# Attention values of the tail keys as 32 by 32 blocks in every chunk of both layers, added on VectorE

## The chip, the cores and the metric

The kernel runs on one core of a Trainium2 chip. The metric is device time in microseconds (us), the median of several runs of the whole program; lower is better.

## The reference

Two layers, each a cross attention and a feed-forward network, gated into a residual stream x of 2 batches by 2048 rows by 512 columns, all in float32:

```python
x = x + tanh(g_xattn[l]) * xattn_l(layernorm(x), ctx)
x = x + tanh(g_ffn[l]) * ffn_l(layernorm(x))
```

The context has 154 keys; there are 16 heads of 32 columns. The first layer's attention has no mask. The second has a mask per query and key and normalises the projected queries, keys and values over 512 columns:

```python
scores = einsum('bhqd,bhkd->bhqk', q, k) / sqrt(32)   # layer 1: where(mask == 0, -1e9, scores)
ctx = einsum('bhqk,bhkd->bhqd', softmax(scores), v)
```

The change touches the product of the softmax with v alone.

## The kernel before

**Tiling.** A layer takes 4096 query rows in 8 chunks of 512 (`NCH`), four per batch; the index of a chunk is `it`, and `it + 1`, `it - 1` are the chunks whose queries and outputs are made beside it. The layer without mask is called plain, the one with mask and head normalisation masked (`norm` in the code). Of the 154 keys 128 are main keys and 26 are tail keys. Heads are taken in four tiles of four (`KT` tiles, `t`; `GH` heads, `j`). A product in float32 precision is three passes of rounded high and low parts (`hi_lo_matmul`, L69); "q0" to "q3" in the prediction are the four tiles of `q_front`, 12 matmuls of 128x512 each. Transposed scores with a main key per partition are "S0" to "S3" (`scores_main`, L1535 and L1538), the products with v "V0" to "V3" (`values_of`, L1552 to L1569), with the softmax sums beside them.

**Tail keys.** `scores_tail` (L1506) makes the tail scores of all 16 heads as 16 blocks of 32 by 32, packed so that a head's 26 tail keys lie in one of four row groups of 32 partitions of one of four tiles; `exps_tail` (L715) on ScalarE (ACT) gives `p_tail`. `keys.v_tail` holds the tail values with zeros where a row belongs to another head, so that `values_of` can take one head's tail with all 128 rows of `p_tail` (L1552), four matmuls of 128 rows by 32 columns, into the PSUM bank `values`, on which the four main products (L1556) are added:

```python
nc.tensor.matmul(values[own, :], keys.v_tail[:, b, t, own], p_tail[:, t, :],
                 start=True, stop=False, skip_group_check=True)
```

`c_evict` (L729, ACT) copies `values` to `c_sb` in SBUF, one tile at a time (there is one `values` bank). VectorE (DVE) multiplies `c_sb` by the reciprocal sums that TensorE (PE) has transposed into two banks (`recips`, L1598; `c_back` L1016 plain, `c_mult` L1025 masked), ACT rounds the high part (`cT_back`, L744), and DVE makes the low part (`c_low`/`lo_of`, L1033). That is the input of the output product `y_back` (L69 with wd).

**PSUM.** Four score banks `score[:, 0..3, :]` are used for S0, S1, S2, S3 in turn, `j` for `j`: a bank is free again when ACT's exponential (`exps_main`, L722) has read it. In the masked layer the banks are first filled with the mask (`seed_main`: j = 0, 1, 2 on DVE, L966, and j = 3 on ACT, L707), and PE accumulates on that. Two banks `bank[0], bank[1]` carry in turn the q tiles, `recips`, `qT_front` and `y_back`; in the masked layer `recips(0,1)` need that DVE has taken q tiles 0 and 1 out of them (`q_rows`, L986).

**The order** is written out by hand, one program per engine, with semaphores. PE's program per chunk, before:

```python
q_front(it + 1, (0,)); scores_main(it, 0); q_front(it + 1, (1,)); scores_main(it, 1)
if norm and it: recips(it - 1, (0, 1))
values_of(it, 0); q_front(it + 1, (2, 3)); scores_main(it, 2); values_of(it, 1)
if norm and it: recips(it - 1, (2, 3))
scores_main(it, 3)
```

Then come V2, V3 and the 16 key-maximum products `max_of` (L1479; masked also L1477), from the third on with a `y_back` group of the chunk before behind each. `max_of` m waits until DVE has reduced max m − 2 (L1009), and the first `y_back` for `c_low` of all four tiles. The max of each query is taken before its exponentials of the next chunk. GpSimd (POOL) widens the reciprocals and adds the gate's bias to a residual tile (`add_bias`, L538); DVE's `mask_front` (L948) unpacks the mask for the maxima.

## Time and profile before

| | |
|---|---|
| median of 3 runs | 2413.8 us (2412.69 to 2415.39) |
| profiled execution, its own time | 2415.25 us |
| its span in the trace | 2413.5 us |
| mean granted TensorE clock | 0.989 |
| busy: DVE, ACT, POOL | 1505.3, 1179.1, 238.7 us |
| a plain chunk from 218.36 us on, a masked chunk from 1360.12 us on | 51.01 us, 54.71 us |

The profile is of one execution, so its rows are set against its own time. Busy times overlap across engines. A row of a timeline gives the start, the busy time of a group of like instructions, the engine, the line and the operation, out<-in; in brackets stands the idle time before it with what ended it. A float32 matmul that is not split leaves two records, so "x8" with L1552 are four matmuls. A granted clock of 1.00 is 2.4 GHz, 0.50 is 1.2 GHz.

### The profile page before, as it was taken

What the parts mean: (1) busy time and instruction counts of PE and PEld (TensorE: products, weight loads), DVE (VectorE), ACT (ScalarE), POOL (GpSimd) and SP (SyncE); (2) the same over time, 40 slices, a digit from 0 to 9 for tenths busy, and PEclk for the clock granted to TensorE, in tenths of its full rate; (3) what the DMA queues carried; (4) which work ended last, traced back from release to release, by engine and by line L of the source; (5) the groups of instructions that cost most, each with busy time, mean ns of one, the idle gap of its engine ahead of it and who ended that gap; (6) DMA issues with size and microseconds to landing.
All of it is one profiled execution on the core that took longest, in us unless ns stands there. A gap on an engine that the chain in (4) does not pass through costs nothing.

```text
span 2413.5 us, 32717 instructions
## 1 busy us (share of the span) xinstructions
PE 2354.9 (98%) x12984; PEld 1795.5 (74%) x12984; DVE 1505.3 (62%) x2466; ACT 1179.1 (49%) x1914; POOL 238.7 (10%) x219
## 2 busy tenths in 40 slices
PE   6999999999999999999988999999999999999998
PEld 5566666688888888888765666666788888888886
DVE  5566666442222222223488888886887988988986
ACT  4454544442222222223245566666666666666665
POOL 1012112210000000000211111113000000000000
PEclk9999999999999999999998999999999999999999
DMA  3121112421101101102311121124301011010110
GB/s 129 36 88 53 53 53 70 162 88 53 35 18 53 52 1 53 53 1 87 121 63 50 67 67 67 67 71 140 110 26 46 36 35 35 36 42 29 36 36 18
DMA packets 89143, 140.95 MB, mean 58 GB/s; under 512 B 5024, under 2 KB 27936, under 8 KB 88992
## 3 DMA queue, kind: packets, MB, share of 16 engines
q1 hardware_dynamic: 88992, 138.87, 17.0%
q8 instruction: 103, 1.69, 0.3%
q14 instruction: 48, 0.39, 0.1%
HBM read 105.30 MB, written 33.55 MB: 58 GB/s over the span
## 4 chain that ended last, share of the span: by engine, by line
PE 39%; DVE 8%; ACT 2%; issue 2%; POOL 0%; DVEq 0%; ACTq 0%
PE l_lay_bank L69 19%; PE l_lay_score L69 11%; PE l_lay_score L1479 1%; PE l_lay_score L1535 1%; PE l_lay_score L1552 1%; DVE l_at_at_next L1084 1%; PE l_lay_score L1556 1%; PE l_lay_score L1564 1%; DVE l_at_h_lo L1098 1%; PE l_lay_bank L1395 1%; DVE l_at_at_next L1077 1%; DVE l_at_full L1073 1%; DVE l_at_full L1066 1%; DVE l_at_xTf_lo L972 1%; DVE l_at_maxes L1009 1%
## 5 line engine op out<-in xcount | busy, mean ns | idle before, releaser
L69 PE MATMUL l_lay_score<-l_at_tw_hi,l_at_h_hi 128*128 128x512 f32 x1024 | 401.4, 392 | 5.2 <-DVE l_at_h_lo L1098 4.7
L69 PE MATMUL l_lay_bank<-l_at_xTf_hi,l_at_tw_hi 128*128 128x512 f32 x1024 | 400.1, 391 | 0.0
L69 PE MATMUL l_lay_score<-l_at_tw_hi,l_at_h_lo 128*128 128x512 f32 x1024 | 398.7, 389 | 0.0
L69 PE MATMUL l_lay_score<-l_at_tw_lo,l_at_h_hi 128*128 128x512 f32 x1024 | 398.5, 389 | 0.0
L69 PE MATMUL l_lay_bank<-l_at_xTf_hi,l_at_tw_lo 128*128 128x512 f32 x1024 | 398.5, 389 | 0.0
L69 PE MATMUL l_lay_bank<-l_at_xTf_lo,l_at_tw_hi 128*128 128x512 f32 x1024 | 398.4, 389 | 0.0
L1058 DVE TENSOR_TENSOR l_at_h_lo<-l_at_full,l_at_h_hi 128x512 fp32r<-128x512 f32 x128 | 94.2, 736 | 468.5 <-ACT l_at_h_hi L762 468.5
L757 ACT ACTIVATE l_at_full<-l_lay_bank,l_at_lay_b 128x512 f32<-128x512 f32 x128 | 88.3, 690 | 457.8 <-PE l_lay_bank L69 457.8
L69 PEld LDWEIGHTS l_lay_score<-l_at_tw_hi,l_at_h_hi 128*128 128x128 f32 x1024 | 192.3, 188 | 49.2 <-DVE l_at_h_lo L1098 10.2
L69 PEld LDWEIGHTS l_lay_score<-l_at_tw_hi,l_at_h_lo 128*128 128x128 f32 x1024 | 192.2, 188 | 40.2
L69 PEld LDWEIGHTS l_lay_bank<-l_at_xTf_hi,l_at_tw_lo 128*128 128x128 f32 x1024 | 192.2, 188 | 40.1
L69 PEld LDWEIGHTS l_lay_bank<-l_at_xTf_hi,l_at_tw_hi 128*128 128x128 f32 x1024 | 192.3, 188 | 40.0 <-issue 0.7
L69 PEld LDWEIGHTS l_lay_bank<-l_at_xTf_lo,l_at_tw_hi 128*128 128x128 f32 x1024 | 192.3, 188 | 39.3
L69 PEld LDWEIGHTS l_lay_score<-l_at_tw_lo,l_at_h_hi 128*128 128x128 f32 x1024 | 192.3, 188 | 38.8
L1009 DVE TENSOR_REDUCE l_at_maxes<-l_lay_score 128x4 f32<-128x616 f32 x256 | 197.7, 798 | 27.6 <-PE l_lay_score L1479 24.9
L722 ACT ACTIVATE l_at_p_main<-l_lay_score 128x512 f32<-128x512 f32 x256 | 131.6, 601 | 106.1 <-PE l_lay_score L1538 106.1
L783 ACT ACTIVATE l_at_at_grid<-l_at_at_grid,l_at_lay_grid_bias 128x512 f32<-128x512 f32 x128 | 92.6, 724 | 149.9 <-DVE l_at_at_grid L1088 149.9
L1479 PE MATMUL l_lay_score<-l_at_k_bd,l_at_qT_hi 128*128 128x308 f32 x512 | 131.8, 343 | 6.2 <-ACT l_lay_score L695 3.3
L769 ACT ACTIVATE l_at_grid<-l_at_full,l_at_lay_grid_bias 128x512 f32<-128x512 f32 x128 | 92.0, 719 | 89.2 <-DVE l_at_full L1066 89.2
L1098 DVE SCALAR_TENSOR_TENSOR l_at_h_lo<-l_at_at_grid,l_at_h_hi 128x512 fp32r<-128x512 f32 x128 | 88.1, 688 | 57.0 <-ACT l_at_h_hi L788 57.0
L669 ACT ACTIVATE l_at_xT_hi<-l_lay_bank 128x512 fp32r<-128x512 f32 x64 | 36.6, 596 | 177.7 <-PE l_lay_bank L1395 177.7
L1479 PEld LDWEIGHTS l_lay_score<-l_at_k_bd,l_at_qT_hi 128*128 128x128 f32 x512 | 95.5, 198 | 36.6 <-DVE l_at_maxes L1009 9.7
(195 smaller groups left out, 4063.2 us busy)
## 6 DMA issues: line engine op xcount, KB each, us to landing
both_x_in<-stream SPq DMA_DIRECT2D x25, 1024.0 KB, 5.6
l_at_xg<-stream SPq DMA_DIRECT2D x23, 1024.0 KB, 5.5
stream<-l_at_xg SPq DMA_DIRECT2D x22, 1024.0 KB, 4.3
l_at_tw_raw<-in_l_w SPq DMA_DIRECT2D x64, 256.0 KB, 5.6
both_x_in<-in_x SPq DMA_DIRECT2D x9, 1024.0 KB, 7.7
l_at_xg<-in_x SPq DMA_DIRECT2D x7, 1024.0 KB, 5.4
out<-l_at_xg SPq DMA_DIRECT2D x7, 1024.0 KB, 4.3
l_at_maskT_in<-in_maskT SPq DMA_DIRECT2D x16, 256.0 KB, 3.2
```

The costliest lines, as they stand in the source:

```text
L69: done = nc.tensor.matmul(out, lhs[a], rhs[b], start=first and n == 0, stop=last and n == len(passes) - 1)
L669: nc.scalar.activation((xT if i < NCH else xTf)[0][:, k, :], (bank if i <= NCH else tr)[k % 2][:, :], ACT.Copy)\
L722: nc.scalar.activation(p_main[:, t % 2, j, :], score[:, j, :], ACT.Exp)\
L757: nc.scalar.activation(full[u % 2][:, :], hid[u % 2][:, :], ACT.Relu, bias=b1[:, u % MT:u % MT + 1]).then_inc(h_full, 1)
L769: nc.scalar.activation(grid[u % 2][:, :], full[u % 2][:, :], ACT.Identity, bias=grid_bias[:, 2:3]).then_inc(gridded, 1)
L783: nc.scalar.activation(at_grid[u % AB][:, :], at_grid[u % AB][:, :], ACT.Identity, bias=grid_bias[:, 3:4]).then_inc(rounded, 1)
L972: nc.vector.tensor_tensor(to[1][:, k, :], ps[k % 2][:, :], to[0][:, k, :].bitcast(F32), ALU.subtract)\
L1009: nc.vector.tensor_reduce(to, heads, AX.X, ALU.max).then_inc(max_done, 1)
L1058: nc.vector.tensor_tensor(h[1][u % HB][:, :], full[u % 2][:, :], h[0][u % HB][:, :].bitcast(F32), ALU.subtract)\
L1066: nc.vector.tensor_scalar(full[u % 2][:, :], hid[u % 2][:, :], b1[:, u % MT:u % MT + 1], ROUND_IN, ALU.add, ALU.add)\
L1098: nc.vector.scalar_tensor_tensor(h[1][u % HB][:, :], at_grid[u % AB][:, :], -ROUND_256, h[0][u % HB][:, :].bitcast(F32), ALU.add, ALU.subt ...
L1479: done = nc.tensor.matmul(to, qT_of(it)[0][:, t, q * P:(q + 1) * P], keys.bd[:, b, t, 2 * a:2 * a + 2, :], start=not norm, stop=True, skip ...
```

## The change

`tail_values(it)` is a new PE step, once per chunk: 16 matmuls of 32 rows by 32 columns, each taking only the row group where its head's tail keys are. Tile 0 goes to the bank `values`, on which V0 then accumulates; tiles 1 to 3 go to score banks 1 to 3. `tail_values_out` copies these to `c_sb`, tile 1 on DVE and 2 and 3 on ACT, before S0 or its seeds may use the banks. `values_of` makes only the main products, and for tiles 1 to 3 `c_add` on DVE replaces `c_evict`: `c_sb = values + c_sb`. In the masked layer the seeds are split two on DVE and two on ACT, and the q rows are taken in halves around the new step. The plain layer has q1 ahead of S0, q2 ahead of S1 and q3 ahead of S2. The last chunks, which have no next queries, get the feed-forward network's first products in the place of q0 and q1, and S0 and S1 stand side by side.

```diff
...
                 act.wait_ge(maskT_done, 2 * it + 2)
-                act.wait_ge(exp_done, NS * it + GH * t + GH)
-                nc.scalar.activation(score[:, GH - 1, :], mask_main[:, it % 2, :], ACT.Copy)\
-                    .then_inc(act_seeded, 1)
+                for j in (2, 3):
+                    act.wait_ge(exp_done, NS * it + GH * t + j + 1)
+                    if t == 0:
+                        act.wait_ge(tail_v_act, 2 * it + j - 1)
+                    nc.scalar.activation(score[:, j, :], mask_main[:, it % 2, :], ACT.Copy)\
+                        .then_inc(act_seeded, 1)
 
...
 
+            def tail_values_out(it, t):
+                act.wait_ge(tail_v_ps, 3 * it + t)
+                if it >= 2:
+                    act.wait_ge(cT_lo, KT * (it - 2) + t + 1)
+                nc.scalar.activation(c_sb[:, it % 2, t, :], score[:, t, :], ACT.Copy).then_inc(tail_v_act, 1)
+
             def c_evict(it, t):
...
                 exps_tail(it)
-                if norm:
-                    seed_main(it, 0)
                 if it < B:
                     v_tail_of(it)
-                if not norm:
+                if norm:
+                    tail_values_out(it, 2)
+                    tail_values_out(it, 3)
+                    seed_main(it, 0)
+                else:
                     if more:
...
                         relu_hi(0)
-                exps_main(it, 0)
-                if norm:
-                    seed_main(it, 1)
-                if not norm:
+                    tail_values_out(it, 2)
+                    tail_values_out(it, 3)
                     if more:
...
                         relu_hi(1)
+                exps_main(it, 0)
+                if norm:
+                    seed_main(it, 1)
+                if more and not norm:
+                    q_front(it + 1, (2,))
                 exps_main(it, 1)
...
                 if more and not norm:
-                    q_front(it + 1, (2, 3))
+                    q_front(it + 1, (3,))
                 exps_main(it, 2)
...
                     seed_main(it, 3)
-                c_evict(it, 1)
                 if it and norm:
...
                     front.round_hi(act, "wd")
-                c_evict(it, 2)
                 if more and norm:
...
                     q_front(it + 1, (1,))
-                c_evict(it, 3)
                 if more and norm:
...
                 dve.wait_ge(maskT_done, 2 * it + 2)
-                for j in range(GH - 1):
+                for j in range(2):
                     dve.wait_ge(exp_done, NS * it + GH * t + j + 1)
+                    if t == 0 and j == 1:
+                        tail_values_out(it, 1)
+                        dve.wait_ge(tail_v_dve, it + 1)
                     nc.vector.tensor_copy(score[:, j, :], mask_main[:, it % 2, :]).then_inc(dve_seeded, 1)
...
 
+            def tail_values_out(it, t):
+                dve.wait_ge(tail_v_ps, 3 * it + t)
+                if it >= 2:
+                    dve.wait_ge(cT_lo, KT * (it - 2) + t + 1)
+                nc.vector.tensor_copy(c_sb[:, it % 2, t, :], score[:, t, :]).then_inc(tail_v_dve, 1)
+
+            def c_add(it, t):
+                c = c_sb[:, it % 2, t, :]
+                if t == 1:
+                    dve.wait_ge(tail_v_dve, it + 1)
+                else:
+                    dve.wait_ge(tail_v_act, 2 * it + t - 1)
+                dve.wait_ge(c_ps, KT * it + t + 1)
+                nc.vector.tensor_tensor(c, values, c, ALU.add).then_inc(c_out, 1)
+
             def c_back(it, ts):
...
                     c = c_sb[:, it % 2, t, :]
+                    dve.wait_ge(c_out, u + 1)
                     dve.wait_ge(rT_ps, u + 1)
...
                     c = c_sb[:, it % 2, t, :]
+                    dve.wait_ge(c_out, KT * it + t + 1)
                     dve.wait_ge(rT_ps, KT * it + t + 1)
...
                         done = hi_lo_matmul(nc, bank[t % 2][:, :], lhs, rhs, k == 0, k == KT - 1)
-                    done.then_inc(q_ps, 1)
+                    if ks[-1] == KT - 1:
+                        done.then_inc(q_ps, 1)
 
...
                         if i == 0:
-                            if not norm:
+                            if not norm and t == 0 and j == 1:
+                                pe.wait_ge(tail_v_dve, it + 1)
+                            elif not norm and t == 0 and j > 1:
+                                pe.wait_ge(tail_v_act, 2 * it + j - 1)
+                            elif not norm:
                                 pe.wait_ge(exp_done, NS * it + GH * t + j + 1)
-                            elif j < GH - 1:
-                                pe.wait_ge(dve_seeded, 3 * (KT * it + t) + j + 1)
                             else:
-                                pe.wait_ge(act_seeded, KT * it + t + 1)
+                                pe.wait_ge(dve_seeded if j < 2 else act_seeded,
+                                           2 * (KT * it + t) + j % 2 + 1)
                         nc.tensor.matmul(score[:, j, :], k2[a][rows[j], b, t, 0:P], q2[c][rows[j], t, :],
...
 
+            def tail_values(it):
+                b = it // CPB
+                pe.wait_ge(exp_done, NS * it + KT)
+                if it:
+                    pe.wait_ge(c_out, KT * it)
+                else:
+                    pe.wait_ge(kv_bias, 8)
+                if it % CPB == 0:
+                    pe.wait_ge(v_placed, V_COPIES * (b + 1))
+                for t in range(KT):
+                    for j in range(GH):
+                        c = own_rows[group_of(t, j)]
+                        to = score[own_rows[j], t, :] if t else values[own_rows[j], :]
+                        done = nc.tensor.matmul(to, keys.v_tail[c, b, t, own_rows[j]], p_tail[c, t, :],
+                                                start=True, stop=t > 0, skip_group_check=True)
+                    if t:
+                        done.then_inc(tail_v_ps, 1)
+
             def values_of(it, t):
...
                     pe.wait_ge(kv_bias, 8)
-                if t == 0 and it % CPB == 0:
-                    pe.wait_ge(v_placed, V_COPIES * (b + 1))
-                for j in range(GH):
-                    own = slice(DH * j, DH * (j + 1))
-                    nc.tensor.matmul(values[own, :], keys.v_tail[:, b, t, own], p_tail[:, t, :],
-                                     start=True, stop=False, skip_group_check=True)
                 for j in range(GH):
...
                                             keys.v_main[:, b, DH * head:DH * (head + 1)],
-                                            p_main[:, t % 2, j, :], start=False, stop=True,
+                                            p_main[:, t % 2, j, :], start=t > 0, stop=True,
                                             skip_group_check=True)
...
                 if more:
-                    q_front(it + 1, (0,))
+                    q_front(it + 1, (0,), (0, 1) if norm else range(KT))
                 else:
                     first_product(0)
-                scores_main(it, 0)
-                if more:
+                tail_values(it)
+                if more and norm:
+                    q_front(it + 1, (0,), (2, 3))
+                    q_front(it + 1, (1,), (0, 1))
+                elif more:
                     q_front(it + 1, (1,))
...
                     first_product(1)
-                scores_main(it, 1)
+                scores_main(it, 0)
+                if more:
+                    q_front(it + 1, (1,) if norm else (2,), (2, 3) if norm else range(KT))
                 if norm and it:
                     recips(it - 1, (0, 1))
+                scores_main(it, 1)
                 values_of(it, 0)
                 if more:
-                    q_front(it + 1, (2, 3))
+                    q_front(it + 1, (2, 3) if norm else (3,))
                 scores_main(it, 2)
```

The rest of the diff does the same for the last chunk, and puts `c_add` into DVE's program, which its order shows.

DVE, masked layer, a middle chunk, from the seeds for S3 (`L966 CAST`, then `L981`) to the first maxima, before:

```order
L966 CAST l_lay_score<-l_at_mask_main 128x512 x3
L1000 TENSOR_SCALAR l_at_qn<-l_at_qn,l_at_lay_q_mv,l_at_lay_q_rstd 128x512 x4
L1025 TENSOR_TENSOR l_at_c_sb<-l_at_c_sb,l_lay_bank 128x512 x2
L1033 TENSOR_TENSOR l_at_xT_lo<-l_at_c_sb,l_at_xT_hi 128x512 x2
L940 TENSOR_SCALAR both_x_in<-both_x_in,l_at_lay_mv,l_at_lay_rstd 128x512 x4
L1033 TENSOR_TENSOR l_at_xT_lo<-l_at_c_sb,l_at_xT_hi 128x512 x2
L980 TENSOR_TENSOR l_at_qT_lo<-l_at_q_0,l_at_qT_hi 128x512
L980 TENSOR_TENSOR l_at_qT_lo<-l_at_q_1,l_at_qT_hi 128x512
L1009 TENSOR_REDUCE l_at_maxes<-l_lay_score 128x4 x7
```

and with the change (`L1015` is `q_norm_apply`, `L1057` `c_mult`, `L1065` `c_low`, `L952` `norm_apply`, `L995` `q_low`, `L1024` a maximum):

```order
L981 CAST l_lay_score<-l_at_mask_main 128x512 x2
L1039 TENSOR_TENSOR l_at_c_sb<-l_lay_score,l_at_c_sb 128x512
L1015 TENSOR_SCALAR l_at_qn<-l_at_qn,l_at_lay_q_mv,l_at_lay_q_rstd 128x512 x4
L1057 TENSOR_TENSOR l_at_c_sb<-l_at_c_sb,l_lay_bank 128x512 x2
L1065 TENSOR_TENSOR l_at_xT_lo<-l_at_c_sb,l_at_xT_hi 128x512 x2
L1039 TENSOR_TENSOR l_at_c_sb<-l_lay_score,l_at_c_sb 128x512
L952 TENSOR_SCALAR both_x_in<-both_x_in,l_at_lay_mv,l_at_lay_rstd 128x512 x4
L1065 TENSOR_TENSOR l_at_xT_lo<-l_at_c_sb,l_at_xT_hi 128x512 x2
L1039 TENSOR_TENSOR l_at_c_sb<-l_lay_score,l_at_c_sb 128x512
L995 TENSOR_TENSOR l_at_qT_lo<-l_at_q_0,l_at_qT_hi 128x512
L995 TENSOR_TENSOR l_at_qT_lo<-l_at_q_1,l_at_qT_hi 128x512
L1024 TENSOR_REDUCE l_at_maxes<-l_lay_score 128x4 x7
```

One cast has gone, and three additions (L1039) stand between the steps ahead of the first maximum.

PE, masked layer, a middle chunk, the second half of q1 to V0, before:

```order
L69 MATMUL l_lay_bank<-l_front_wq_hi,l_at_xT_hi 128x512
L69 MATMUL l_lay_bank<-l_front_wq_lo,l_at_xT_hi 128x512
L69 MATMUL l_lay_bank<-l_front_wq_hi,l_at_xT_lo 128x512
L1535 MATMUL l_lay_score<-l_at_qT_hi,l_at_k_hi 128x512 x4
L1535 MATMUL l_lay_score<-l_at_qT_lo,l_at_k_hi 128x512 x4
L1535 MATMUL l_lay_score<-l_at_qT_hi,l_at_k_lo 128x512 x4
L1538 MATMUL l_lay_score<-l_at_negT,l_at_pick 128x512 x4
L1598 MATMUL l_lay_bank<-ident,l_at_r_wide 128x128 x8
L1552 MATMUL l_lay_score<-l_at_p_tail,l_at_v_tail 32x512 x4
L1556 MATMUL l_lay_score<-l_at_p_main,l_at_v_main 32x512 x4
L1564 MATMUL l_lay_score<-l_at_p_main,l_at_e_main 32x512 x4
```

and with the change (`L1586`, `L1589` are `scores_main`, `L1661` `recips`):

```order
L69 MATMUL l_lay_bank<-l_front_wq_hi,l_at_xT_hi 128x512
L69 MATMUL l_lay_bank<-l_front_wq_lo,l_at_xT_hi 128x512
L69 MATMUL l_lay_bank<-l_front_wq_hi,l_at_xT_lo 128x512
L1661 MATMUL l_lay_bank<-ident,l_at_r_wide 128x128 x8
L1586 MATMUL l_lay_score<-l_at_qT_hi,l_at_k_hi 128x512 x4
L1586 MATMUL l_lay_score<-l_at_qT_lo,l_at_k_hi 128x512 x4
L1586 MATMUL l_lay_score<-l_at_qT_hi,l_at_k_lo 128x512 x4
L1589 MATMUL l_lay_score<-l_at_negT,l_at_pick 128x512 x4
L1619 MATMUL l_lay_score<-l_at_p_main,l_at_v_main 32x512 x4
L1627 MATMUL l_lay_score<-l_at_p_main,l_at_e_main 32x512 x4
```

`recips` has moved ahead of S1, and the tail product (L1552) has gone from V0.

DVE, plain layer, a middle chunk, from `norm_apply` to the maxima, before:

```order
L940 TENSOR_SCALAR both_x_in<-both_x_in,l_at_lay_mv,l_at_lay_rstd 128x512 x4
L1016 TENSOR_TENSOR l_at_c_sb<-l_at_c_sb,l_lay_bank 128x512 x2
L1033 TENSOR_TENSOR l_at_xT_lo<-l_at_c_sb,l_at_xT_hi 128x512 x2
L1016 TENSOR_TENSOR l_at_c_sb<-l_at_c_sb,l_lay_bank 128x512 x2
L1033 TENSOR_TENSOR l_at_xT_lo<-l_at_c_sb,l_at_xT_hi 128x512 x2
L1009 TENSOR_REDUCE l_at_maxes<-l_lay_score 128x4 x8
```

and with the change (`L1047` is `c_back`):

```order
L952 TENSOR_SCALAR both_x_in<-both_x_in,l_at_lay_mv,l_at_lay_rstd 128x512 x4
L1039 TENSOR_TENSOR l_at_c_sb<-l_lay_score,l_at_c_sb 128x512
L1047 TENSOR_TENSOR l_at_c_sb<-l_at_c_sb,l_lay_bank 128x512 x2
L1065 TENSOR_TENSOR l_at_xT_lo<-l_at_c_sb,l_at_xT_hi 128x512 x2
L1039 TENSOR_TENSOR l_at_c_sb<-l_lay_score,l_at_c_sb 128x512
L1047 TENSOR_TENSOR l_at_c_sb<-l_at_c_sb,l_lay_bank 128x512 x2
L1065 TENSOR_TENSOR l_at_xT_lo<-l_at_c_sb,l_at_xT_hi 128x512 x2
L1024 TENSOR_REDUCE l_at_maxes<-l_lay_score 128x4 x3
L1039 TENSOR_TENSOR l_at_c_sb<-l_lay_score,l_at_c_sb 128x512
L1024 TENSOR_REDUCE l_at_maxes<-l_lay_score 128x4 x5
```

The three additions stand ahead of the first `c_back`, between the two, and behind the third maximum.

## Rows read from the trace of the kernel before

**Rows 1.** The page, busy time by engine
```profile
PE 2354.9 (98%) x12984; PEld 1795.5 (74%) x12984; DVE 1505.3 (62%) x2466; ACT 1179.1 (49%) x1914; POOL 238.7 (10%) x219
```

**Rows 2.** Windows, one steady chunk of each layer: us, busy and count by engine, clock, DMA
```profile
218.36:269.37 51.01, 50.95 (x377) 33.78 (x376) 32.50 (x50) 23.19 (x42) 8.15 (x7) 1.00 0.17 63
1360.12:1414.83 54.71, 54.58 (x418) 36.05 (x417) 47.75 (x82) 33.18 (x58) 9.73 (x9) 1.00 0.22 75
```

**Rows 3.** Timeline of PE, plain chunk: start, busy time of the group, instruction
```profile
220.01 1.14 PE L1506 MATMUL l_lay_score<-l_at_q,l_at_k_tail 32*32 32x512 f32 x32
221.08 1.09 PE L1395 MATMUL l_lay_bank<-ident,both_x_in 128*128 128x128 f32 x8
231.59 0.40 PE L1538 MATMUL l_lay_score<-l_at_negT,l_at_pick 32*128 32x512 f32 x4
231.92 1.07 PE L1552 MATMUL l_lay_score<-l_at_p_tail,l_at_v_tail 128*32 128x512 f32 x8
232.80 1.04 PE L1556 MATMUL l_lay_score<-l_at_p_main,l_at_v_main 128*32 128x512 f32 x8
241.14 0.51 PE L1535 MATMUL l_lay_score<-l_at_qT_hi,l_at_k_hi 32*128 32x512 f32 x4
```

**Rows 4.** Timeline of ACT, DVE and PE, same chunk, its second half
```profile
242.59 2.04 ACT L722 ACTIVATE l_at_p_main<-l_lay_score 128x512 f32<-128x512 f32 x4
246.29 2.06 ACT L722 ACTIVATE l_at_p_main<-l_lay_score 128x512 f32<-128x512 f32 x4 [1.16 <-PE l_lay_score L1538]
250.55 1.28 DVE L1016 TENSOR_TENSOR l_at_c_sb<-l_at_c_sb,l_lay_bank 128x512 f32<-128x512 f32 x2 [0.36 <-PE l_lay_bank L1598]
251.94 1.29 DVE L1033 TENSOR_TENSOR l_at_xT_lo<-l_at_c_sb,l_at_xT_hi 128x512 fp32r<-128x512 f32 x2
253.15 2.40 DVE L1009 TENSOR_REDUCE l_at_maxes<-l_lay_score 128x4 f32<-128x616 f32 x3
254.16 0.55 PE L1479 MATMUL l_lay_score<-l_at_k_bd,l_at_qT_hi 128*128 128x308 f32 x2
```

**Rows 5.** Timeline of PE, masked chunk: q row 2, max 2
```profile
1378.68 0.49 PE L69 MATMUL l_lay_bank<-l_front_wq_hi,l_at_xT_hi 128*128 128x512 f32 x1
1399.04 0.30 PE L1477 MATMUL l_lay_score<-l_at_mask_add,ident_bf 128*128 128x308 bf16 x1
```

**Rows 6.** Timeline of DVE and POOL, masked chunk
```profile
1370.85 1.88 DVE L966 CAST l_lay_score<-l_at_mask_main 128x512 f32<-128x512 bf16 x3 [0.46 <-ACT l_at_p_main L722]
1373.06 0.69 DVE L986 TENSOR_TENSOR l_at_qn<-l_lay_bank,l_at_q_rows 128x512 f32<-128x512 f32 x1 [0.33 <-PE l_lay_bank L69]
1374.40 2.05 DVE L948 TENSOR_SCALAR l_at_mask_add<-l_at_mask_in 128x616 bf16<-128x616 int32 x1
1395.73 1.29 DVE L1033 TENSOR_TENSOR l_at_xT_lo<-l_at_c_sb,l_at_xT_hi 128x512 fp32r<-128x512 f32 x2 [1.16 <-ACT l_at_xT_hi L744]
1398.18 2.43 DVE L1009 TENSOR_REDUCE l_at_maxes<-l_lay_score 128x4 f32<-128x616 f32 x3
1371.52 4.58 POOL L538 TENSOR_TENSOR l_at_xg<-l_at_xg,l_at_gate_bias 128x2048 f32<-128x2048 f32 x1 [2.17 <-DMA l_at_xg<-stream]
```

**Rows 7.** Timeline of ACT and PE, first masked chunk
```profile
1253.44 1.66 ACT L662 ACTIVATE l_at_v_tail<-l_at_v_nat 32x32 f32<-32x32 f32 x8
1270.42 2.06 ACT L722 ACTIVATE l_at_p_main<-l_lay_score 128x512 f32<-128x512 f32 x4 [7.15 <-PE l_lay_score L1538]
1272.58 0.60 ACT L707 ACTIVATE l_lay_score<-l_at_mask_main 128x512 f32<-128x512 bf16 x1
1272.97 0.75 PE L1535 MATMUL l_lay_score<-l_at_qT_hi,l_at_k_hi 32*128 32x512 f32 x4
```

**Rows 8.** Timeline of PE, first plain chunk
```profile
100.61 1.06 PE L1552 MATMUL l_lay_score<-l_at_p_tail,l_at_v_tail 128*32 128x512 f32 x8 [1.11 <-ACT l_at_c_sb L729]
```

**Rows 9.** Windows at the first chunk's maxima, columns as above
```profile
100.00:110.00 10.00, 7.74 (x42) 3.73 (x42) 6.84 (x10) 1.67 (x3) 0.00 (x0) 0.93 0.00 0
110.00:114.00 4.00, 3.70 (x10) 2.40 (x10) 3.40 (x6) 0.00 (x0) 0.00 (x0) 0.50 0.01 4
```

More of the change, by code:

```diff
@@ L314, in layer_phase @@
         seeded = n.sem("seeded")
+        tail_v_ps, tail_v_dve, tail_v_act = (n.sem(s) for s in ("tail_v_ps", "tail_v_dve", "tail_v_act"))
         dve_seeded, act_seeded = n.sem("dve_seeded"), n.sem("act_seeded")
@@ L956, in maskT_front @@
                     if it >= 2 and i:
-                        dve.wait_ge(act_seeded, KT * (it - 1))
-                        dve.wait_ge(dve_seeded, 3 * KT * (it - 1))
+                        dve.wait_ge(act_seeded, 2 * KT * (it - 1))
+                        dve.wait_ge(dve_seeded, 2 * KT * (it - 1))
                     nc.vector.tensor_scalar(to, maskT_in[:, i, :], 0, -BIG, ALU.is_equal,
@@ L1241, in _ @@
                     seed_main(it, 3)
+                    c_add(it, 1)
                     q_norm_apply(it + 1)
                 else:
+                    tail_values_out(it, 1)
                     q_low(it + 1, (0, 1))
@@ L1247, in _ @@
                     norm_apply(it + 2)
+                    c_add(it, 1)
                 if it and norm:
@@ L1252, in _ @@
                     c_back(it - 1, (0, 1))
+                c_add(it, 2)
                 if norm:
@@ L1259, in _ @@
                 if norm:
+                    c_add(it, 3)
                     q_low(it + 1, (0, 1))
@@ L1262, in _ @@
                     max_of(it + 1, m)
+                    if m == 2 and not norm:
+                        c_add(it, 3)
                     if m in (6, 9) and norm:
@@ L1279, in _ @@
                     round_hidden(u)
-                else:
-                    relu_lo(u)
+            if not norm:
+                tail_values_out(last, 1)
+                relu_lo(0)
+                relu_lo(1)
+                c_add(last, 1)
             if norm:
@@ L1285, in _ @@
                 seed_main(last, 3)
+                c_add(last, 1)
                 c_low(last - 1, (0, 1))
                 c_mult(last - 1, (2, 3))
+                c_add(last, 2)
                 c_low(last - 1, (2, 3))
+                c_add(last, 3)
             else:
                 c_back(last - 1, (0, 1))
+                c_add(last, 2)
                 c_back(last - 1, (2, 3))
+                c_add(last, 3)
             y_back(last - 1, 0)
@@ L1424, in kT_front, with q_front @@
                                         ident[0:SLOT, 0:SLOT]).then_inc(kT_ps, 1)
-            def q_front(it, ts):
+            def q_front(it, ts, ks=range(KT)):
                 if it == 0:
@@ L1434, in q_front @@
                             pe.wait_ge(c_normed, KT * (it - 2) + t - 1)
-                    for k in range(KT):
+                    for k in ks:
                         if norm:
```

## The prediction

> **What bounds the kernel now.** I read the page's busy times first: TensorE (PE) is busy for 98% of the span [rows 1], so the first idea is that PE time saved is time saved. Then the table of windows over one steady chunk of each layer: PE works 50.95 of 51.01 us in the plain layer and 54.58 of 54.71 us in the masked one, and VectorE (DVE) 32.50 and 47.75 us [rows 2]. PE is full in both, but in the masked layer DVE has only 7 us of slack. Last the timelines, at the places where one engine hands to another. They show that PE arrives at the third key-maximum product (max 2, which waits until DVE has reduced max 0) just as DVE is ready. In the plain chunk DVE begins max 0 at 253.15 and PE begins max 2 at 254.16, 0.15 us later than the 0.86 us it takes from that start in the masked chunk, where they are 1398.18 and 1399.04 [rows 4, 6]. So PE and the chain DVE, ScalarE (ACT), DVE behind the last scores end together. A saving on PE alone ends as idle time before max 2; what decides is what the change does to that chain.
>
> **PE's own work, per chunk.** Four calls of `values_of` each lose four tail matmuls; those start 0.88 us before the main ones (231.92 to 232.80) [rows 3]: −3.52 us. Added is `tail_values`, 16 matmuls of 32 by 32 in four groups of four. No row shows four different weights in both directions. The nearest is the tail scores, 32 records in the trace for 16 matmuls of 32 by 32, which take 1.07 us (220.01 to 221.08) [rows 3]. Its bounds are the four groups at one stream each, 0.88 us, and 16 matmuls with no overlap at 0.22 us each, the same 3.52 us that were removed. I take 1.07, the row of the same shape. One more boundary between shapes costs about 0.1 us: the next form starts 0.33 us after the last pass of the scores (231.59 to 231.92) where one stream takes 0.22 us [rows 3]. Net −3.52 + 1.07 + 0.1 = **−2.35 us**, 16 chunks −37.6 us. The Trainium skill ("TensorEngine Tiling (Array Packing)", Key Properties) says that changing the tiling mode drains TensorE; by that rule each boundary costs a drain, and the 0.1 us above is what this trace shows of it.
>
> **Plain layer, chunks 1 to 6.** The order of PE is now q0, tail values, q1, S0, q2, S1, V0, q3, S2, V1, S3. Tail values add 1.07 ahead of S2 and V0 gives back 0.88; with boundaries S2 starts 0.42 us later and S3 0.46 us earlier on PE's account. But S3 needs the banks that ACT's exponentials of S2 free, and those begin about 1.45 us after S2 (242.59 against 241.14) [rows 3, 4] and free the last bank four steps of 0.51 later. So S3 can't use its 0.46 us: exps 3 begin at 246.29 as before, `cT_back` at 248.21 too. Copying tail values out costs DVE one step early in the chunk and ACT two, both in idle time (ACT waits 1.16 us before exps 3 and gives up three `c_evict`) [rows 4]. What hurts is the order on DVE: `c_add(2)` stands between `c_back(0,1)` and `c_back(2,3)`, the latter having 0.36 us of idle ahead of it [rows 4] and a further 0.11 us between its end (251.83) and `c_low(2,3)` (251.94). One DVE step is 0.60 us (two take 1.28, of which a single one's 0.68). 0.60 − 0.36 − 0.11 = +0.13 us for max 0, and PE had 0.15 us to spare: **0 per chunk** (−0.05 to +0.35). PE's 2.35 us turn into idle time, mostly before max 2. `c_add(3)` behind max 2 is covered while PE runs ahead by several banks.
>
> **Plain edges.** In the first chunk PE waited 1.11 us for ACT's eviction of values 2, behind the rounding of wd [rows 8]. That wait goes with the eviction, and the DVE-paced maxima begin sooner: −2.1 us. In the last chunk S0 and S1 stand next to each other, so S1 waits for exps 0, and the later ones follow that pace: +1.9 us. Layer: −0.2 us.
>
> **Masked layer, chunks 2 to 6.** The S1 banks must be seeded with the mask by DVE (0 and 1) and ACT (2 and 3), after exps 0. Before, ACT did one seed after four exponentials, now two: one more ACT step of about 0.54 us in series. The first chunk shows what a late seed does: exps 2 at 1270.42, ACT's seed at 1272.58, PE's S3 at 1272.97 with its first group stretched to 0.75 us while it waits (the same group takes 0.51 us at 241.14) [rows 3, 7]. From these rows: exps start + 2.16 is the first seed, + 0.54 the second, + 0.39 PE. At the same time DVE's order holds `q_rows(1)` until the seeds for S1 are done; it was at 1373.06 [rows 6]. `recips(0,1)`, now ahead of S1 and using the bank that `q_rows(0/1)` free, waits with it. I get about 1.07 us of PE idle ahead of S1, and `q2` starts 1.26 us later than at 1378.68 [rows 5].
>
> Further down, DVE's chain: `q_rows(3)` +0.71 (part of the 1.26 is covered, since DVE had no need of q3's end before), one seed less −0.59, wait for the last bank of exps 2 +0.19, `c_add(1)` +0.60, `c_add(2)` +0.60; the 1.16 us of idle ahead of `c_low(2,3)` (1395.73) [rows 6] and 0.05 us of smaller gaps are used up, −1.21; `c_add(3)` +0.60. Together 0.71 − 0.59 + 0.19 + 0.60 + 0.60 − 1.21 + 0.60 = **+0.90 us** for max 0, and PE starts max 2 0.86 us after it as now [rows 5, 6]. The four seeds that DVE gives up (0.59 us each: three take 1.88) [rows 6] lie early but for one; its three adds lie on the chain that counts. `mask_front` (2.05 us) ends with GpSimd's `add_bias` (1371.52 + 4.58 = 1376.10; 1374.40 + 2.05 = 1376.45) [rows 6], so that moving it a little costs nothing. Five chunks: +4.5 us, with 0 and 2 us per chunk as ends.
>
> **Masked edges.** In the first chunk tail values wait for eight `v_tail` copies on ACT (1.66 us) [rows 7], and the two outputs and two seeds come behind them: +1.7 us. In chunk 1 the same walk gives −0.3, because `mask_front` already holds the middle of that chunk up. The last chunk, S0 and S1 close together with seeds between: +1.4 us. Layer: 1.7 − 0.3 + 4.5 + 1.4 = **+7.3 us**.
>
> **Sum.** −0.2 + 7.3 = +7.1 us. The profiled execution took 2415.25 us (span 2413.5), so 2422.4; it stands 1.45 us above the median of 2413.8, so the forecast for the median is **2421 us**.
>
> **Rivals.**
> 1. *PE-bound, full gain*: the DVE chain is not the end, max 2 follows PE. 2413.8 − 37.6 = 2376 us. For it: PE at 98%. Against: max 0 and max 2 touch in both layers [rows 4, 6]. 0.07.
> 2. *Gain in the plain layer only*: DVE there works 32.50 of 51.01 us [rows 2], and if the exponentials are not what starts S3's chain, 8 × 2.35 = 18.8 us come off, and the masked 7.3 are added: 2402 us. 0.12.
> 3. *Nothing*: S3 uses its 0.46 us in the plain layer (−2.8), and the masked seeds and `q_rows(1)` don't hold up S1, which takes 0.9 us per chunk off: −0.2 − 2.8 + 7.3 − 4.5, about 2414 us. 0.18. The forecast's own share is 0.46.
> 4. *The clock*: the new idle time before max 2, about 1.4 us per chunk, stands at the beginning of the maxima, where PE has narrow products. In the window 100 to 110 us PE is busy for 7.74 of 10 us and in the next four the granted clock is 0.50, the lower level, 1.2 GHz [rows 9]; otherwise it is at 2.4 GHz. If some 12 of the 16 chunks each get such a stretch of 3.4 us at half speed, of which 1.7 us are lost, that is +20 us on top: 2441 us. It decides from the point where idle time in one stretch is as in that window; steady chunks had none, so no row excludes it. 0.17.
>
> The Trainium skill's "TensorEngine Tiling (Array Packing)", PSUM Bottleneck, warns that tiling speeds up TensorE but not the evacuation of PSUM, and advises both other engines for it. The kernel's chain agrees: what is saved is PE, and one copy and one add per group is new evacuation.
>
> **Chances and range.** A measurement of this kernel can tell about 0.2%, 4.8 us, from no change: the bounds are 2409.0 and 2418.6. Faster: rivals 1 and 2, 0.19, and 0.07 of rival 3 and of the low end of the forecast: 0.26. Same: 0.13 of rival 3 and 0.13 of the forecast (masked chunks at less than +0.4 each): 0.26. Slower: the rest of the forecast and rival 4: 0.48. The range reaches from rival 2 to rival 4, 2402 to 2441; the forecast's own is 2414 to 2428. Left out are rival 1 and the tails.
>
> **What would show it.** Right: in a steady chunk PE idles 1.3 to 1.5 us before max 2 with DVE's max 0 named as releaser; periods of 51.0 and 55.6 us; PE's busy sum lower by 30 to 40 us; an idle of about 1 us before the masked S1 or `recips`; tail values 1.07 us from start to start. Wrong: a plain period below 50 (rivals 1, 2), a masked one at 54.7 or less (3), granted clock 0.5 in windows of steady chunks (4), or tail values of over 2 us, by which PE's saving itself would be gone.

## The result and the profile after

| | before | with the change |
|---|---|---|
| median of 9 runs | 2414.1 us | 2420.9 us |
| ratio of the change to before | | 1.0027, 95% interval 1.0018 to 1.0036 |
| profiled execution, span | 2413.5 us | 2418.8 us |
| PE busy | 2354.9 us | 2333.6 us |
| DVE, ACT busy | 1505.3, 1179.1 us | 1511.5, 1188.7 us |

The change costs 6.8 us by the medians, 5.3 us by the two profiled spans, which have the same mean granted clock, 0.989. Part of the 6.8 us may be the clock: the executions with the change run from 2412.6 us at a mean of 0.994 to 2421.8 us at 0.989. The predicted time was 2421 us. PE's busy sum is 21.3 us lower and the kernel is longer: a case of work taken off an engine that is busy for 98% of the span, without a gain.

The page after, first line of the busy times, answers to [rows 1]:

```profile
PE 2333.6 (96%) x12984; PEld 1786.2 (74%) x12984; DVE 1511.5 (62%) x2498; ACT 1188.7 (49%) x1930; POOL 241.6 (10%) x219
```

The windows of the same two steady chunks (columns as in [rows 2]):

```profile
216.01:266.92 50.91, 49.50 (x378) 33.23 (x377) 33.77 (x55) 22.63 (x41) 8.80 (x7) 1.00 0.17 63
1360.89:1416.47 55.58, 52.95 (x419) 35.55 (x418) 47.45 (x83) 34.67 (x61) 9.74 (x9) 1.00 0.22 73
```

A plain chunk takes 50.91 us where it took 51.01, a masked one 55.58 us where it took 54.71. PE's idle time went from 0.06 to 1.41 us and from 0.13 to 2.63 us, at a granted clock of 1.00. The timeline of PE in these chunks names where it stands (the brackets hold the idle time and its releaser; L1527 and L1525 are max 2, L1661 `recips`, L1619 V3):

```profile
251.29 0.55 PE L1527 MATMUL l_lay_score<-l_at_k_bd,l_at_qT_hi 128*128 128x308 f32 x2 [1.28 <-DVE l_at_maxes L1024]
...
1375.88 0.30 PE L1661 MATMUL l_lay_bank<-ident,l_at_r_wide 128*128 128x128 f32 x1 [0.80 <-DVE l_at_qn L1001]
...
1394.80 1.06 PE L1619 MATMUL l_lay_score<-l_at_p_main,l_at_v_main 128*32 128x512 f32 x8 [0.35 <-DVE l_at_c_sb L1039]
...
1400.25 0.30 PE L1525 MATMUL l_lay_score<-l_at_mask_add,ident_bf 128*128 128x308 bf16 x1 [1.42 <-DVE l_at_maxes L1024]
```

Before the change none of these waits was there in the two chunks. The list of PE's waits over the whole program (total us, times, longest) had 3.9 and 2.2 us behind DVE's maxima; now:

```profile
PE l_lay_score L1525 <- DVE l_at_maxes L1024: 13.1, 11, 1.9
PE l_lay_score L1527 <- DVE l_at_maxes L1024: 10.1, 11, 1.3
...
PE l_lay_bank L1661 <- DVE l_at_qn L1001: 4.8, 6, 0.8
...
PE l_lay_score L1619 <- DVE l_at_c_sb L1039: 3.5, 8, 0.7
```

The chain that sets the masked period is DVE's. Its timeline from the last q row (L1001) to max 0 (L1024) names no idle time at all (some parts are left out below); L1039 are the three additions:

```profile
1386.07 0.69 DVE L1001 TENSOR_TENSOR l_at_qn<-l_lay_bank,l_at_q_rows 128x512 f32<-128x512 f32 x1
...
1387.95 1.29 DVE L981 CAST l_lay_score<-l_at_mask_main 128x512 f32<-128x512 bf16 x2
1389.15 0.68 DVE L1039 TENSOR_TENSOR l_at_c_sb<-l_lay_score,l_at_c_sb 128x512 f32<-128x512 f32 x1
...
1393.96 0.70 DVE L1039 TENSOR_TENSOR l_at_c_sb<-l_lay_score,l_at_c_sb 128x512 f32<-128x512 f32 x1
1394.56 1.92 DVE L952 TENSOR_SCALAR both_x_in<-both_x_in,l_at_lay_mv,l_at_lay_rstd 128x512 f32<-128x512 f32 x4
1396.38 1.30 DVE L1065 TENSOR_TENSOR l_at_xT_lo<-l_at_c_sb,l_at_xT_hi 128x512 fp32r<-128x512 f32 x2
1397.58 0.70 DVE L1039 TENSOR_TENSOR l_at_c_sb<-l_lay_score,l_at_c_sb 128x512 f32<-128x512 f32 x1
1398.18 1.30 DVE L995 TENSOR_TENSOR l_at_qT_lo<-l_at_q,l_at_qT_hi 128x512 fp32r<-128x512 f32 x2
1399.38 2.44 DVE L1024 TENSOR_REDUCE l_at_maxes<-l_lay_score 128x4 f32<-128x616 f32 x3
```

`c_low(2,3)` (L1065) had 1.16 us of idle ahead of it [rows 6] and has none. Max 0 starts 0.86 us later than it did, measured from the transposes of the maxima, with which I begin a chunk (1399.38 − 1360.89 = 38.49 us, against 1398.18 − 1360.55 = 37.63 us), and max 2 waits for it. The chain starts with PE: the last q row begins 0.43 us after PE's last matmul of q tile 3 (1385.64), and in the next chunk DVE waits 1.00 us for that tile.

### The profile page after: what moved, and what is told of

Its sections match the earlier page's. It is cut to its first block, busy times and chain, and to the rows that moved or that the text cites. A ratio compares the mean times of both kernels' runs of the same rounds, so it can differ in the third digit from the quotient of the medians.

```text
span 2418.8 us, 32910 instructions
## 1 busy us (share of the span) xinstructions
PE 2333.6 (96%) x12984; PEld 1786.2 (74%) x12984; DVE 1511.5 (62%) x2498; ACT 1188.7 (49%) x1930; POOL 241.6 (10%) x219
## 4 chain that ended last, share of the span: by engine, by line
PE 36%; DVE 11%; ACT 2%; issue 1%; POOL 0%; DVEq 0%; ACTq 0%
PE l_lay_bank L69 18%; PE l_lay_score L69 11%; PE l_lay_score L1527 1%; DVE l_at_at_next L1116 1%; PE l_lay_score L1586 1%; DVE l_at_h_lo L1130 1%; DVE l_at_at_next L1109 1%; DVE l_at_full L1098 1%; PE l_lay_bank L1442 1%; DVE l_at_full L1105 1%; DVE l_at_xTf_lo L987 1%; DVE l_at_maxes L1024 1%; DVE l_lay_score L981 1%; DVE l_at_xT_lo L1065 1%; DVE both_x_in L952 1%
## 5 line engine op out<-in xcount | busy, mean ns | idle before, releaser
L1024 DVE TENSOR_REDUCE l_at_maxes<-l_lay_score 128x4 f32<-128x616 f32 x256 | 196.8, 798 | 18.2 <-PE l_lay_score L1527 15.2
L1527 PE MATMUL l_lay_score<-l_at_k_bd,l_at_qT_hi 128*128 128x308 f32 x512 | 132.2, 343 | 13.6 <-DVE l_at_maxes L1024 10.1
L1527 PEld LDWEIGHTS l_lay_score<-l_at_k_bd,l_at_qT_hi 128*128 128x128 f32 x512 | 95.8, 198 | 44.6 <-DVE l_at_maxes L1024 19.3
```

Of the source, the lines that this page charges most:

```text
L1024: nc.vector.tensor_reduce(to, heads, AX.X, ALU.max).then_inc(max_done, 1)
L1527: done = nc.tensor.matmul(to, qT_of(it)[0][:, t, q * P:(q + 1) * P], keys.bd[:, b, t, 2 * a:2 * a + 2, :], start=not norm, stop=True, skip ...
```

## The experiments

My theory: the period of a chunk is set by a chain through DVE and ACT that starts at the last q row and the last scores and ends at max 0; PE's work ahead of that start counts, PE's work behind it does not until the idle time before max 2 is used up. The rivals were that PE's time counts everywhere, that it counts nowhere while PE idles, and that other waits (ACT's seeds, q's low parts) set the chain. "Period" is the distance between the same step of PE (the transposes of the maxima) in two neighbouring steady chunks of the profiled execution. Times are medians; the ratio is to before, with its 95% interval. All runs are of the changed kernel with an edit, unless said otherwise.

**PE work behind the last scores.**

```diff
             def values_of(it, t):
...
+                if t == KT - 1:
+                    for j in range(GH):
+                        own = slice(DH * j, DH * (j + 1))
+                        nc.tensor.matmul(values[own, :], keys.v_tail[:, b, t, own], p_tail[:, t, :],
+                                         start=True, stop=True, skip_group_check=True)
```

> The changed kernel with four of the old tail matmuls (128 rows by 32 columns, 0.88 us together) put back in V3 of every chunk, where their result is overwritten by the main product. V3 lies between the last scores and max 2. My theory (max 2 waits for DVE's chain; PE has 1.28 us of idle time ahead of it in a plain chunk and 1.42 us in a masked one): a steady chunk does not get longer, its idle time before max 2 shrinks to 0.4 and 0.5 us; only the two last chunks and the first pay, +1 to +3 us in all, about 2423. If PE's time counts wherever it is spent: +0.88 us in each of 16 chunks, 2435.

Measured: 2420.4 us, ratio 1.0030 (1.0018 to 1.0042); periods 50.9 and 55.5 us, as without the edit. The same two places of PE's timeline:

```profile
250.13 0.56 PE L1527 MATMUL l_lay_score<-l_at_k_bd,l_at_qT_hi 128*128 128x308 f32 x2 [0.42 <-DVE l_at_maxes L1024]
...
1399.76 0.30 PE L1525 MATMUL l_lay_score<-l_at_mask_add,ident_bf 128*128 128x308 bf16 x1 [0.56 <-DVE l_at_maxes L1024]
```

The idle time fell by 0.86 us and the period did not grow. Over a third of the 2.35 us that the change took off PE per chunk can be given back for nothing. That PE's time counts everywhere (2435 us) has fallen. The 1 to 3 us that I expected in the first and last chunks don't show: the median is 0.5 us lower, the profiled span 0.2 us longer.

**PE work ahead of the last scores.**

```diff
                     for k in ks:
...
+                        if it and t == KT - 1 and k == 0:
+                            hi_lo_matmul(nc, bank[t % 2][:, :], lhs, rhs, True, True)
```

> The changed kernel with one of the twelve-matmul q tile 3's four groups issued twice (three matmuls of 128x512, 0.69 us; the second start overwrites the first) in 14 chunks. It lies ahead of S2. My theory (what counts of PE is what stands ahead of the last scores and of DVE's last q row, from which the chain to max 0 starts): +0.69 us in every chunk, the idle time before max 2 stays at 1.28 and 1.42 us, +9.7 us, about 2431. Rival (the idle time before max 2 takes up PE work wherever it stands in the chunk): 0, 2421. Second rival, for the masked layer alone (DVE is full there and does not wait for q tile 3): +0.69 in 7 plain chunks only, +4.8 us.

Measured: 2429.9 us, ratio 1.0069 (1.0056 to 1.0081), 9.0 us above the changed kernel; periods 51.6 and 56.3 us, +0.7 in both layers. The idle time before max 2 is what it was:

```profile
254.94 0.55 PE L1529 MATMUL l_lay_score<-l_at_k_bd,l_at_qT_hi 128*128 128x308 f32 x2 [1.28 <-DVE l_at_maxes L1024]
...
1404.66 0.30 PE L1527 MATMUL l_lay_score<-l_at_mask_add,ident_bf 128*128 128x308 bf16 x1 [1.41 <-DVE l_at_maxes L1024]
```

So 0.69 us costs its full price at one place of the chunk and 0.88 us nothing at another, with the same idle time behind both. The second rival, that the masked DVE doesn't wait for q tile 3, has fallen too.

**The masks two and two.** `seed_main` with three casts on DVE and one on ACT, the waits counted accordingly:

```diff
-                for j in range(2):
+                for j in range(3):
...
-                for j in (2, 3):
+                for j in (3,):
```

> The changed kernel with the score masks split as before, three on DVE and one on ACT. My theory (DVE's order holds q_rows(1) behind the seeds for S1 and c_add behind the seeds for S3): +0.6 us at recips and S1 and +0.6 us behind the last q row, about +1.2 us in each of 7 masked chunks, masked period 56.8, +8 us, 2429. Rival (S1 and S3 wait for ACT's second seed, which this takes away): 0 to -0.5 us per chunk, 2417 to 2421.

Measured: 2427.1 us, ratio 1.0054 (1.0041 to 1.0068), 6.2 us above; masked period 56.75 us, +1.15. `recips` waits 1.39 us (0.80), V3 1.24 us (0.35), and max 2 still 1.41. The split itself is worth 1.15 us per masked chunk: without it the change would cost about twice as much. In this direction ACT's second seed holds nothing up.

**The third addition out of the chain.**

```diff
                 if norm:
-                    c_add(it, 3)
                     q_low(it + 1, (0, 1))
...
-                    if m == 2 and not norm:
+                    if m == 2:
                         c_add(it, 3)
```

> The changed kernel with the masked layer's third addition (c_add of tile 3) behind max 2, as the plain layer has it, and not ahead of max 0. My theory (each addition ahead of max 0 costs its 0.60 us): -0.60 us in each of 7 masked chunks, masked period 55.0, about 2417. Rival (ACT's rounding of q tiles 0 and 1, for which DVE's q_low waits ahead of max 0, sets the time, not the addition): -0.2 us per chunk or less, 2420 to 2421.

Measured: 2421.8 us, ratio 1.0031 (1.0021 to 1.0041); masked period 55.6 us, no gain. My expectation missed; the rival's number holds, but not its reason. Max 2 did come 0.6 us earlier (its wait is 0.82 us), but a new wait stands behind it. PE and ACT there:

```profile
1400.24 0.30 PE L1524 MATMUL l_lay_score<-l_at_mask_add,ident_bf 128*128 128x308 bf16 x1 [0.82 <-DVE l_at_maxes L1024]
1403.33 0.53 PE L1526 MATMUL l_lay_score<-l_at_k_bd,l_at_qT_hi 128*128 128x308 f32 x2 [0.39 <-ACT l_lay_score L696]
```

```profile
1402.49 1.29 ACT L696 ACTIVATE l_lay_score<-l_at_mask_add 128x616 f32<-128x616 bf16 x2 [1.53 <-DVE l_at_c_sb L1039]
```

From max 4 on the masked maxima use a third pair of banks, and that pair is `values` and `sums`. `seed_max(4)` on ACT (L696) therefore waits for `c_add(3)`, at 1402.49 where it had started at 1400.48. The addition is free neither ahead of max 0 nor behind max 2. Whether it would be free directly behind max 0 was not tried.

**The plain chain earlier.**

```diff
                 if norm and it:
                     recips(it - 1, (2, 3))
+                elif it and more:
+                    recips(it - 1, (0, 1))
                 scores_main(it, 3)
                 if it and not norm:
-                    recips(it - 1, (0, 1))
+                    recips(it - 1, (2, 3) if more else (0, 1))
                 values_of(it, 2)
...
-                if it and norm:
+                if it and (norm or more):
                     cT_back(it - 1, (0, 1))
                 exps_main(it, 3)
...
-                    c_back(it - 1, (0, 1))
+                    c_mult(it - 1, (0, 1))
+                    c_mult(it - 1, (2, 3))
+                    c_low(it - 1, (0, 1))
                 c_add(it, 2)
```

> The changed kernel with the plain layer's chain to max 0 begun earlier: recips(0,1) ahead of S3 and recips(2,3) ahead of V2 on PE, cT_back(0,1) ahead of the last exponentials on ACT, both multiplications ahead of the low parts on DVE; the masked layer as it is. My theory (that chain, not PE, sets the plain period; PE has 1.28 us of idle time before max 2 and some 0.56 us of stretch in S3): -1.0 to -1.8 us in each of 6 chunks, plain period 49.1 to 49.9, about 2413. Rival (the maxima themselves or S3's exponentials are the limit): the period stays at 50.9, 2421.

Measured: 2411.7 us, ratio 0.9991 (0.9981 to 1.0000); plain period 49.7 us, −1.2. The wait before max 2 is gone; PE waits 0.23 us, for the multiplications before `recips(2,3)`.

**The masked DVE load moved.**

```diff
                     if t == 0 and j == 1:
+                        if it and it < last:
+                            maskT_front(it + 1)
                         tail_values_out(it, 1)
...
-                    q_rows_front(it + 1, (2, 3))
+                    q_rows_front(it + 1, (2,))
+                    norm_apply(it + 2)
+                    q_rows_front(it + 1, (3,))
...
+                if it and norm:
+                    cT_back(it - 1, (2, 3))
                 if more and norm:
                     q_front(it + 1, (0,))
```

(`norm_apply`, `maskT_front` and `cT_back(2,3)` go from their old places.)

> The changed kernel with DVE's load moved in the masked layer: mask transposes of the next chunk into the idle time ahead of the tail copy, norm_apply between q rows 2 and 3, and on ACT cT_back(2,3) ahead of the q tiles; the plain layer as it is. My theory (what stands on DVE between the last q row and max 0 costs its own time up to PE's idle 1.42 us): -1.0 to -1.45 us in each of 7 chunks, masked period 54.1 to 54.6, 2411 to 2414. Rival (from add3_late: the masked maxima are a chain of their own between DVE and ACT that doesn't begin earlier): period 55.5, 2420.

Measured: 2413.1 us, ratio 0.9992 (0.9983 to 1.0001); masked period 54.5 us, −1.1. Max 2 no longer waits; V3's wait for `c_add(2)` is 0.62 us in the place of 0.35. So the masked maxima do begin earlier when the whole chain does; it was only the third pair of banks that `add3_late` held back.

**Both orders, and the same orders without the change.**

> The changed kernel with the edits of plain_recips and masked_order together. The layers are apart, so the gains add: about 2404, under both kernels. If they work only by accident of one layer's clock or transfers, the sum is less: 2412.

> The kernel before the change with the same orders as far as they apply (recips and cT_back early in the plain layer, norm_apply between q rows 2 and 3 and cT_back(2,3) early in the masked). My theory (PE is full there, so an earlier chain gives nothing, and only together with the change does it): 2413 to 2415, within 0.1% of before. Rival (the orders are a gain by themselves): 2400 to 2408.

Measured: both orders 2406.5 us, ratio 0.9961 (0.9945 to 0.9976), and once more, below, 2401.6 us: the same kernel, two medians 5 us apart. Both orders together are 0.4% faster than before.

Before with part of the orders took 2418.5 us, ratio 1.0022 (1.0013 to 1.0030), with periods of 51.2 and mostly 55.6 to 56.0 us. My expectation of 2413 to 2415 missed. The run isn't a full counterpart of `both_orders`: `norm_apply` stands ahead of the last q row as there, but `maskT_front` was not moved to make room for it. The last q row and the seeds behind it come 1.97 us later in the chunk, and the first group of S3, which took 0.51 us, waits for its seeds:

```profile
1383.46 1.58 PE L1537 MATMUL l_lay_score<-l_at_qT_hi,l_at_k_hi 32*128 32x512 f32 x4
```

So these orders without the change are slower. That the kernel before can't be made faster by any other order is not shown; against it stands only that PE is full there [rows 2]. The windows of both orders:

```profile
212.19:261.94 49.75, 49.38 (x379) 33.01 (x377) 33.65 (x55) 22.49 (x41) 8.91 (x7) 1.00 0.18 64
1343.48:1397.97 54.49, 53.01 (x419) 35.47 (x417) 46.47 (x83) 34.23 (x61) 9.53 (x9) 1.00 0.21 75
```

PE's idle time is down to 0.37 us in the plain chunk and 1.48 us in the masked one. No engine's busy time in these windows moved by 1 us; what moved is the order.

**The second addition ahead of the low parts, and the last plain chunk.** The first edit, in the masked layer:

```diff
                     c_mult(it - 1, (2, 3))
+                    c_add(it, 2)
                     c_low(it - 1, (0, 1))
...
-                c_add(it, 2)
+                if not (it and norm):
+                    c_add(it, 2)
```

The second, on top of it, in the last plain chunk:

```diff
-                    first_product(1)
+                    first_product(1, range(KT) if norm else (0, 1))
                 scores_main(it, 0)
+                if not more and not norm:
+                    first_product(1, (2, 3))
...
+                exps_main(it, 0)
+                if not more and not norm:
+                    relu_hi(1)
```

> both_orders again, so that the three stand beside each other: as before, about 2406.

> both_orders with the second addition on DVE ahead of c_low(0,1) in the masked layer. There PE has no idle time before max 2 any more, but V3 waits 0.62 us for c_add(2). My theory (with the chain to max 0 out of the way PE's own waits count): -0.4 to -0.6 us in each of 7 masked chunks, masked period 53.9 to 54.1, 3 to 4 us under both_orders measured beside it. Rival (max 0 then is late by the same, DVE being full): the wait moves to max 2 and the period stays at 54.5.

> add2_early with the last plain chunk in another order: S0 between the halves of the feed-forward network's second first product and its exponentials ahead of ACT's relu of that product, so that S1 no longer follows S0 at once. In the trace of the changed kernel that S1 waits 0.89 us and is stretched to three times its time. My theory (this is most of what the last plain chunk costs): -1.5 to -2.5 us against add2_early. Rival (ACT's late relu holds up the later exponentials as long): 0.

Measured side by side: both orders 2401.6 us, ratio 0.9961 (0.9946 to 0.9977); with the second addition earlier 2400.8 us, 0.9952 (0.9934 to 0.9969); with the last chunk split as well 2400.7 us, 0.9948 (0.9932 to 0.9964). The masked period goes from 54.5 to 54.0 us, −0.45, as expected; V3 doesn't wait, and max 2 waits 0.29 us, once 0.37. The last plain chunk, from the maxima's transposes to the `recips` behind it, goes from 43.95 us in both kernels without the split to 42.55 us. The second addition was expected to give 3 to 4 us and gives 0.8 us by the medians, 2.7 us by the spans of the two executions with a mean clock of 0.994 (2397.0 and 2394.3 us); the split was expected to give 1.5 to 2.5 us and gives 0 by the medians, 1.4 us by the trace. So those gains are read from the traces alone; the intervals of the three ratios overlap, so the times don't separate them. The best version by the traces is the last one; its median is 0.5% under before.

## Why the prediction was right

The mechanism was right, and most of its steps. That 2421 and 2420.9 us agree to 0.1 us is luck: the forecast was +7.1 us over before, the profiled spans at equal mean clock differ by 5.3 us, and by the parts below the plain layer came to +0.6 us for −0.2 and the masked one to +5.1 for +7.3, with some of the clock in both. Taken by the same marks in both traces, in us:

| part | forecast | measured |
|---|---|---|
| plain, first chunk | −2.1 | −1.5 |
| plain, second chunk | 0 | −0.8 |
| plain, five more, each | 0 | −0.1 |
| plain, last chunk | +1.9 | +3.3 |
| masked, first chunk | +1.7 | +1.8 |
| masked, second chunk | −0.3 | −1.4 |
| masked, steady, each | +0.9 | +0.8 to +0.9 in four, 0 in one |
| masked, last chunk | +1.4 | +1.4 |
| idle before max 2, plain and masked | 1.3 to 1.5 | 1.28 and 1.42 |
| q2's start in the masked chunk | +1.26 | +1.28 |

- *What bounds the kernel.* Right: PE, and beside it a chain that ends at max 0. `v3_pad` and `q3_pad` show it from both sides, and `both_orders` shows that with the chain shortened the idle time goes and the kernel is 0.4% faster than before.
- *PE's own work.* Tail values take 1.14 us busy, as the tail scores, and 1.08 us from their start (223.91) to that of q1 behind them (224.99), where 1.07 were assumed. The PE sum fell by 21.3 us, less than the 30 to 40 forecast as a sign of it: a group's modelled busy time is longer than its step (1.07 against 0.88 us for the old tail group [rows 3]), and stretched groups such as S3 count as busy (its first group takes 1.06 us in the plain chunk for 0.51). The busy sum is the wrong measure of a saving; the distance between starts is the right one.
- *Plain steady chunks.* Right, 0 forecast, −0.1 measured. `c_add(2)` stands where it was said to.
- *Masked steady chunks.* The sum was right (0.90 against 0.86 for max 0), with one reason in it wrong and one too large. The forecast had S1 held up by ACT's second seed; S1 starts unstretched (0.51 us for its first group). The wait is at `recips`, 0.80 us where the forecast had 1.07. Its reason, that DVE's order holds `q_rows(1)` behind the seeds, holds for about half of that:

```profile
1373.85 1.29 DVE L981 CAST l_lay_score<-l_at_mask_main 128x512 f32<-128x512 bf16 x2 [1.60 <-ACT l_at_p_main L726]
1375.05 0.68 DVE L1001 TENSOR_TENSOR l_at_qn<-l_lay_bank,l_at_q_rows 128x512 f32<-128x512 f32 x1
```

  PE's last matmul of q tile 1 starts at 1374.25. Before the change DVE's q row began 0.43 us after that matmul (1372.63 to 1373.06); here it begins 0.80 us after it, straight behind the seeds. So 0.37 us of the wait is the seeds, and 0.43 us is the way PE, DVE, PE, which was behind S1 before. `seeds_3_1` agrees: the third seed adds 0.59 us. One steady chunk (the last but one) got no longer because before the change it already waited 0.81 us for `c_mult` at q2.
- *`mask_front`.* Moving it was said to cost nothing, and it even became shorter: 2.05 us before and 1.68 with the change in the chunk shown, 1.74 and 0.71 in the next. It ends about 0.3 us behind GpSimd's `add_bias` in all four, whenever it starts.
- *Edges.* The plain ones were off by 1.4 us at the most, and part of what is off is the clock. In the last plain chunk the profiled execution has a stretch at the lower clock (below). Without it, in the executions of `both_orders`, `both_again` and `add2_early`, with the same order of PE in that chunk, it takes 43.95 to 43.99 us against 42.27 before: +1.7, and the forecast was +1.9. The other 1.6 us is the clock. The second plain chunk's −0.8 is the clock too: before the change the clock is at the lower level for its first 3.5 us, with the change for its first 1.4 us, and the 0.8 us are gained there. The first two plain chunks together, with the whole of that stretch in both executions, come to −2.3 us for −2.1. In the second masked chunk the stretches at the lower clock lie elsewhere in the two executions as well, so its −1.4 isn't a clean measure. In that chunk `mask_front` took 4.40 us before and 0.72 with the change.
- *Rivals.* The clock rival has fallen as it was put: 1.28 and 1.42 us of idle before max 2 leave the granted clock at 1.00 in the steady chunks shown. Its remark that the clock is otherwise at 2.4 GHz was too wide: the execution before the change has lower stretches in other places too, three of them named below. "Full gain" and "plain gain only" have fallen with the plain period of 50.9 us and with `v3_pad`; "nothing" has fallen with the masked period of 55.6 us.

The Trainium skill ("TensorEngine Tiling (Array Packing)", PSUM Bottleneck) says that tiling doesn't speed up evacuation. The traces agree as far as they go: the additions of 0.60 us each stand in a chain without idle time. But the busy sums of DVE and ACT rose by 6.2 and 9.6 us only, and `both_orders` has the same evacuations and is faster; it was their place in the order that held the saving back.

## What to carry to other kernels

When an engine is full and a chain through the others ends beside it, find the point from which the chain starts. Time taken off the full engine behind that point becomes a wait; work added ahead of it costs its whole price. An edit that takes PE work away and adds a step to the chain needs the chain shortened in the same edit, else it reads as a failure: here the change alone cost 0.3%, and with the chain shortened in both layers the kernel was 0.4% faster than before. Test it with pads of the same size on either side of the supposed start, two runs that need no theory to read.

## What the runs showed of the hardware

Between executions the granted clock falls at different places. In the last plain chunk of the changed kernel S1 waits 0.89 us for ACT, and its first group takes 1.86 us while it waits further for its banks. In `both_orders` the same S1 waits the same 0.89 us and its first group takes 1.87 us. Behind it the two differ. In the changed kernel's execution the clock is at the lower level (1.2 GHz) in the window 436 to 438 us, and V0 takes 1.94 us; in that of `both_orders` the clock stays at 1.00 and V0 takes 1.06 us:

```profile
432.00:434.00 2.00, 1.11 (x17) 0.59 (x13) 0.78 (x1) 1.97 (x4) 2.00 (x1) 1.00 0.23 87
436.00:438.00 2.00, 2.00 (x13) 0.41 (x13) 0.00 (x0) 1.58 (x4) 2.00 (x1) 0.50 0.00 0
```

```profile
436.67 1.94 PE L1619 MATMUL l_lay_score<-l_at_p_main,l_at_v_main 128*32 128x512 f32 x8
```

The 0.89 us is also shorter than the waits before max 2, behind which the clock did not fall. Stretches at the lower clock late in the plain layer's feed-forward network come and go in the same way: three before the change (near 1184, 1208 and 1228 us), two with it (near 1183 and 1228 us), none in `both_orders`. `plain_recips` and `both_orders` have the same plain layer. The distance from its last maxima transposes to the masked layer's first ones was 826.7 us in the profiled execution of the one, at a mean clock of 0.990, and 820.8 us in that of the other, at 0.994. It is 6 us between executions of programs that are the same there, as much as this change is worth, so single spans were compared by parts, and whole times only by their medians.
